# Seven block products over pairs of tiles in place of eight in two graph aggregations, and a first stage whose input comes in column layout

## The reference

```python
def _L1_gnn_ref(x, adj, W, b):
    agg = jnp.matmul(adj, x)
    out = jnp.matmul(agg, W.T) + b
    return jax.nn.relu(out)

def _L3_gnn_ref(x, adj, W, b):
    a = adj + jnp.eye(adj.shape[0], dtype=adj.dtype)
    d = jnp.sum(a, axis=1) ** (-0.5)
    a_norm = d[:, None] * a * d[None, :]
    support = a_norm @ x
    out = support @ W.T + b
    return jax.nn.relu(out)
...
x = _layernorm(x + _L1_gnn_ref(x, adj, L1_gnn_W, L1_gnn_b), axis=-1)
```

## Time and profile before

| | us |
|---|---|
| median of three runs | 2541.1 |
| lowest and highest | 2539.39, 2542.22 |
| the profiled execution, its own time | 2541.41 |
| its span, first to last instruction | 2539.6 |

### The profile page before, as it was taken

How to read it: one execution, slowest core, us unless ns; L and a number is a source line. 1 busy time by engine, 2 the same in 40 slices (tenths; PEclk the granted TensorE clock), 3 DMA queues, 4 the chain that set the end, 5 groups by cost and what they waited for, 6 DMA issues and landing times. The chain is left out here.

```text
span 2539.6 us, 67049 instructions
## 1 busy us (share of the span) xinstructions
PE 2424.1 (95%) x24988; PEld 1557.7 (61%) x24988; DVE 1545.9 (61%) x3013; ACT 1364.0 (54%) x2036; POOL 1148.7 (45%) x971
## 2 busy tenths in 40 slices
PE   7997999999999999999879997999999999979998
PEld 6885777777777777777634443774444555534443
DVE  4435998898888898888632222555555566633222
ACT  3335888888888888888623221324434444323222
POOL 0005888888888888888601232001111113310323
PEclk9998999999999999999989999999999999989999
DMA  3216999999999999999743654215666779733664
GB/s 130 65 62 129 183 195 185 188 193 181 190 193 178 187 193 184 191 188 185 123 137 118 213 199 158 100 37 138 175 183 181 203 207 233 178 128 101 211 213 140
DMA packets 783644, 417.41 MB, mean 164 GB/s; under 512 B 691296, under 2 KB 717664, under 8 KB 774496
## 3 DMA queue, kind: packets, MB, share of 16 engines
q1 hardware_dynamic: 783456, 414.62, 70.7%
HBM read 203.55 MB, written 40.84 MB: 96 GB/s over the span
## 5 line engine op out<-in xcount | busy, mean ns | idle before, releaser
L806 DVE CUSTOM_DVE_ANT_0 att_scores<-att_slots,att_adj 128x1024 f32<-128x1024 f32 x528 | 575.7, 1091 | 41.6 <-POOL att_part_low L627 14.5
L627 POOL TENSOR_TENSOR att_part_low<-att_scores,att_part_high 128x1024 f16<-128x1024 f32 x352 | 574.8, 1651 | 12.0 <-ACT att_part_high L790 1.1
L751 ACT ACTIVATE att_scores<-att_scores,att_nmax 128x1024 f32<-128x1024 f32 x528 | 552.4, 1047 | 28.2 <-DVE att_lifted L817 26.0
L672 PE MATMUL att_slots<-l_kk,att_q 128*128 128x512 f16 x2112 | 466.5, 356 | 15.5 <-DMA att_q<-q_rows 8.9
L1345 PE MATMUL a_ps<-l_y,a_adj 128*128 128x512 f16 x1936 | 421.2, 381 | 9.0 <-DVE a_adj L1359 4.7
L825 DVE TENSOR_TENSOR att_near_low<-att_ps_t,att_near_high 128x512 f16<-128x512 f32 x528 | 316.4, 599 | 37.6 <-ACT att_near_high L760 35.9
L760 ACT ACTIVATE att_near_high<-att_ps_t 128x512 f16<-128x512 f32 x528 | 258.2, 524 | 150.0 <-PE att_ps_t L682 137.3
L1345 PEld LDWEIGHTS a_ps<-l_y,a_adj 128*128 128x128 f16 x1936 | 190.0, 98 | 240.1 <-DVE a_adj L1359 5.2
L672 PEld LDWEIGHTS att_slots<-l_kk,att_q 128*128 128x128 f16 x2112 | 195.2, 98 | 173.4 <-DVE att_least L806 24.9
L1090 PE MATMUL edge_ps_o<-l_sup,edge_pt_high 128*128 128x512 f16 x968 | 287.9, 379 | 1.7 <-DMA edge_pt_low<-edge_part_low 1.7
L1330 ACT ACTIVATE a_adj<-l_adj 128x2816 f16<-128x2816 f32 x44 | 112.0, 2549 | 291.1 <-DMA l_adj<-in_adj_cols 271.1
(11 more groups left out here) (152 smaller groups left out, 3863.2 us busy)
## 6 DMA issues: line engine op xcount, KB each, us to landing
l_adj<-in_adj_cols SPq DMA_DIRECT2D x44, 1408.0 KB, 6.1
l_adj_tiles<-in_adj SPq DMA_DIRECT2D x22, 1354.0 KB, 6.1
att_adj<-in_adj SPq DMA_DIRECT2D x66, 384.0 KB, 4.2
p_x_in<-x SPq DMA_DIRECT2D x66, 256.0 KB, 2.6
att_q<-q_rows SPq DMA_DIRECT2D x44, 256.0 KB, 3.8
a_xres<-x SPq DMA_DIRECT2D x44, 256.0 KB, 2.8
p_x_in<-in_x SPq DMA_DIRECT2D x22, 256.0 KB, 2.7
q_rows<-l0w_q_halves SPq DMA_DIRECT2D x22, 256.0 KB, 2.1
```

Source lines behind the costliest of these rows:

```text
L627: nc.gpsimd.tensor_tensor(out=part[1][:, v, lo:lo + width], in0=sc[:, v, lo:lo + width], in1=part[0][:, v, lo:lo + width], op=ALU.subtract ...
L672: mm = nc.tensor.matmul(slots[:, slot, z:z + w], q[:, u, h % 2, a, h // 2, :], kk[:, h, lo + z:lo + z + w], start=a == 0, stop=a == 1)
L751: nc.scalar.activation(sc[:, v, lo:lo + width], sc[:, v, lo:lo + width], ACT.Exp, bias=nmax[:, v:v + 1], scale=-1.0).then_inc(exp_done, 1)
L806: nc.vector.tensor_tensor_reduce(out=sc[:, v, lo:lo + width], in0=slots[:, (NC * h + c) % 2, 0:width], in1=adj[:, u, lo:lo + width], scale ...
```

## The change

`aggregate` works on pairs of output tiles, m = 0 to 10. A pair's adjacency columns are a 2x2 grid by parity of the block and tile in the pair, y a 2x2 grid by parity of the tile and half of the columns. By Strassen's scheme seven products of block sums give the four quarters. ACT narrows both tiles of a pair into one of three buffers, DVE makes five sums of blocks (`combine`, each 11 blocks of 128, 1408 elements), PE runs seven products of 22 matmuls with 256 columns each, ACT copies four of the products from PSUM to SBUF, DVE puts the quarters together (`add`, eight additions of 256 columns), then come bias, residual and statistics of both tiles (`bias`). The second factor, seven combinations of quarters of y with high and low part, is made in p1 and p3: ACT evicts both tiles of a pair in float32 (`y32`), DVE makes the five sums, ACT and DVE write the high and low parts (`halves`). The loops of p1, p3, a1 and a3 are written out. In p0 the host gives x in column layout (`x_cols`): no transposes, ACT and DVE split it straight out of the loaded tile, and the second tile of x is loaded behind the key weights, ahead of the others.

```diff
+def each(eng, begin, end, step):
+    for t in range(begin, end):
+        step(t // 2, t % 2)
...
+                src = x_rows[bass.ds((2 * m + u), 1), :, :].rearrange("o p n -> (o p) n") if columns \
+                    else x_rows[bass.ds((2 * m + u) * P, P), :]
+                sp.dma_start(x_in[:, u, :], src).then_inc(x_loaded[u], 16)
...
             load(0, 0)
-            own.load(sp)
+            own.load(sp, slice(0, 2))
             load(0, 1)
+            own.load(sp, slice(2, None))
             late_w.load(sp)
...
+                if columns:
+                    return
...
+                        if combos is None:
+                            pe.wait_ge(out_low, nj * (2 * m + u - 2) + n + 1)
+                        else:
+                            pe.wait_ge(evicted, 2 * m + u - 1)
...
+            def halves(m, u):
+                t = 2 * m + u
+                act.wait_ge(made, t + 1)
+                if t > 1:
+                    act.wait_ge(out_low, 2 * m)
+                scale = V_S * XW if row_scale is None else row_scale[:, bass.ds(t, 1)]
+                slots = y32[:, 1::2, :] if u == 0 else y32[:, 0::2, :]
+                nc.scalar.activation(slots, ps_job[0][:, u, :].rearrange("p (c n) -> p c n", c=2), ACT.Copy,
+                                     scale=scale).then_inc(evicted, 1)
+                if u == 1:
+                    act.wait_ge(evicted, t + 1)
+                    nc.scalar.activation(combos[0][:, 5:7, m, :], y32[:, 1:3, :], ACT.Copy).then_inc(out_high, 1)
+                    act.wait_ge(y_summed, 3 * m + 3)
+                    nc.scalar.activation(combos[0][:, 0:5, m, :], sums[:, :, :], ACT.Copy).then_inc(out_high, 1)
...
+            def halves(m, u):
+                if u == 0:
+                    return
+                dve.wait_ge(evicted, 2 * m + 2)
+                if m > 0:
+                    dve.wait_ge(out_low, 2 * m)
+                nc.vector.tensor_tensor(out=sums[:, 0:2, :], in0=y32[:, 0:2, :], in1=y32[:, 2:4, :], op=ALU.add) \
+                    .then_inc(y_summed, 1)
+                nc.vector.tensor_tensor(out=sums[:, 2:4, :], in0=y32[:, 0:4:3, :], in1=y32[:, 1:3, :],
+                                        op=ALU.subtract).then_inc(y_summed, 1)
+                nc.vector.tensor_tensor(out=sums[:, 4, :], in0=y32[:, 1, :], in1=y32[:, 2, :], op=ALU.add) \
+                    .then_inc(y_summed, 1)
+                dve.wait_ge(out_high, 2 * m + 1)
+                nc.vector.tensor_tensor(out=combos[1][:, 5:7, m, :], in0=y32[:, 1:3, :], in1=combos[0][:, 5:7, m, :],
+                                        op=ALU.subtract).then_inc(out_low, 1)
+                dve.wait_ge(out_high, 2 * m + 2)
+                nc.vector.tensor_tensor(out=combos[1][:, 0:5, m, :], in0=sums[:, :, :], in1=combos[0][:, 0:5, m, :],
+                                        op=ALU.subtract).then_inc(out_low, 1)
...
-        a16 = s.sb("adj16", [P, 2, T, P], F16)
+        a16 = s.sb("adj16", [P, 3, 2, T, P], F16)
+        a_sum = s.sb("adj_sum", [P, 2, 5, T // 2, P], F16)
         xres = s.sb("xres", [P, 2, D])
-        act_in = s.sb("act_in", [P, D])
+        total, copied = s.sb("total", [P, 2, 2, D // 2]), s.sb("copied", [P, 2, 2, D // 2])
         norm = Norm(s)
-        ps = s.ps("ps", [P, 2, BANK])
+        ps = s.ps("ps", [P, 2, 4, 2, D // 2])
...
+            def load_adj(t):
+                if t > 1:
                     sp.wait_ge(narrowed, t - 1)
+                    sp.dma_start(a32[:, t % 2, :, :], columns_of(adj_cols, t)).then_inc(adj_loaded[t % 2], 16)
+            def load_x(t):
+                if t > 1:
                     sp.wait_ge(r_ready, t - 1)
+                sp.dma_start(xres[:, t % 2, :], x_rows[t * P:(t + 1) * P, :]).then_inc(xres_loaded[t % 2], 16)
+            load_adj(2)
+            load_adj(3)
+            load_x(0)
+            load_x(1)
+            for m in range(1, M):
+                if m < M - 1:
+                    load_adj(2 * m + 2)
+                    load_adj(2 * m + 3)
+                for u in range(2):
+                    load_x(2 * m + u)
+                    norm.store(sp, out_rows, m - 1, u)
+            norm.store(sp, out_rows, M - 1, 0)
+            norm.store(sp, out_rows, M - 1, 1)
...
+            def narrow(m):
+                for u in range(2):
+                    if m > 0:
+                        act.wait_ge(adj_loaded[u], 16 * m)
+                    if m > 2:
+                        act.wait_ge(summed, PRODUCTS * (m - 2))
+                    nc.scalar.activation(a16[:, m % 3, u, :, :], a32[:, u, :, :], ACT.Copy).then_inc(narrowed, 1)
+            for m in range(3):
+                narrow(m)
+            for m in range(M):
+                for n in range(2):
+                    act.wait_ge(summed, PRODUCTS * m + 2 + 4 * n)
+                    if m > 0:
+                        act.wait_ge(added, ADDS * m)
+                    nc.scalar.activation(copied[:, n, :, :], ps[:, m % 2, 2 * n, :, :], ACT.Copy) \
+                        .then_inc(copies, 1)
+                if m + 3 < M:
+                    narrow(m + 3)
...
+            for m in range(M):
+                pe.wait_ge(combined, 4 * (m + 1))
+                if m > 1:
+                    pe.wait_ge(added, ADDS * (m - 1))
+                s16, s2 = a16[:, m % 3, :, :, :], a_sum[:, m % 2, :, :, :]
+                a11, a22 = s16[:, 0, 0::2, :], s16[:, 1, 1::2, :]
+                factors = [(s2[:, 4, :, :], 4), (a22, 2), (s2[:, 0, :, :], 6), (s2[:, 2, :, :], 0),
+                           (a11, 3), (s2[:, 1, :, :], 5), (s2[:, 3, :, :], 1)]
+                for n, (a, c) in enumerate(factors):
+                    for k in range(M):
+                        for b in range(2):
+                            mm = nc.tensor.matmul(ps[:, m % 2, n // 2, n % 2, :], a[:, k, :], y[b][:, c, k, :],
+                                                  start=k == 0 and b == 0, stop=k == M - 1 and b == 1)
+                    mm.then_inc(summed, 1)
...
+            def combine(m):
+                s16, out = a16[:, m % 3, :, :, :], a_sum[:, m % 2, :, :, :]
+                dve.wait_ge(narrowed, 2 * m + 2)
+                if dcol is not None:
+                    for u in range(2):
+                        block_of = s16[:, u, 2 * m + u, :]
+                        nc.vector.tensor_tensor(out=block_of, in0=block_of, in1=ident[:, :], op=ALU.add) \
+                            .then_inc(diag_ready, 1)
+                    dve.wait_ge(diag_ready, 2 * m + 2)
+                if m > 1:
+                    dve.wait_ge(summed, PRODUCTS * (m - 1))
+                for u in range(2):
+                    op_of = nc.vector.tensor_tensor(out=out[:, u, :, :], in0=s16[:, u, 0::2, :],
+                                                    in1=s16[:, u, 1::2, :], op=ALU.add)
+                op_of.then_inc(combined, 1)
+                for n, (u, odd, v, odder, op) in enumerate(((0, 1, 1, 1, ALU.subtract), (1, 0, 0, 0, ALU.subtract),
+                                                            (0, 0, 1, 1, ALU.add))):
+                    nc.vector.tensor_tensor(out=out[:, 2 + n, :, :], in0=s16[:, u, odd::2, :],
+                                            in1=s16[:, v, odder::2, :], op=op).then_inc(combined, 1)
+            def add(m):
+                m5, m7, m6 = (ps[:, m % 2, n // 2, n % 2, :] for n in (2, 3, 6))
+                m1, m4, m3, m2 = (copied[:, n // 2, n % 2, :] for n in range(4))
+                c11, c12, c21, c22 = (total[:, n // 2, n % 2, :] for n in range(4))
+                if m > 0:
+                    dve.wait_ge(r_ready, 2 * m)
+                for n, (made, out, a, b, op, own) in enumerate((
+                        (2, c11, m1, m4, ALU.add, 0), (4, c11, c11, m5, ALU.subtract, 1), (4, c11, c11, m7, ALU.add, 2),
+                        (6, c12, m3, m5, ALU.add, 0), (6, c21, m2, m4, ALU.add, 0), (6, c22, m1, m2, ALU.subtract, 0),
+                        (6, c22, c22, m3, ALU.add, 6), (7, c22, c22, m6, ALU.add, 7))):
+                    dve.wait_ge(copies, 2 * m + (1 if made < 6 else 2))
+                    dve.wait_ge(summed, PRODUCTS * m + made)
+                    if own:
+                        dve.wait_ge(added, ADDS * m + own)
+                    nc.vector.tensor_tensor(out=out, in0=a, in1=b, op=op).then_inc(added, 1)
+            def bias(m, u):
+                t = 2 * m + u
+                scale = 1.0 / V_S if dcol is None else dcol[:, t:t + 1]
+                row = total[:, u, :, :].rearrange("p c n -> p (c n)")
+                dve.wait_ge(added, ADDS * m + (5 if u == 0 else ADDS))
+                nc.vector.scalar_tensor_tensor(out=row, in0=row, scalar=scale, in1=bias_row[:, :], op0=ALU.mult,
+                                               op1=ALU.add).then_inc(biased, 1)
                 dve.wait_ge(biased, t + 1)
                 dve.wait_ge(xres_loaded[u], 16 * m + 16)
                 norm.free(dve, m, u)
```

(21 more changed lines are left out.)

111 lines of the change are left out of this document (32 added, 79 removed).

## The result

The changed kernel takes 2800.9 us (median of four runs, 2795.86 to 2804.34), the kernel before in the same comparison 2541.3. The ratio is 1.102, with a 95% interval from 1.100 to 1.104: slower by 260 us. The profiled execution of it spans 2797.9 us, against 2539.6.

The account below looks back on a forecast made before the run. PE bound the kernel before; after, a serial ring of queues would pace the aggregations. From 2541.4 us, +179 for the aggregations with their ends, +56 for the projections and -14 for the first stage gave 2762, range 2720 to 2840.

Parts of the forecast that it names:

- PE gives back 24 us per aggregation: Aggregations: eleven pairs of 256-column matmuls take PE 185 us against 209, if nothing else sets the pace.
- The ring: Aggregations: store, next loads, narrowing, copies, adds, biases and block sums follow in series, 30.0 us per pair; PE needs 16.8.
- The last term, bias to store: Aggregation's ring: second tile's bias, statistics, POOL and the store's issue take 6.04 us, read from the earlier trace.
- A block sum of 0.89 us: Aggregations: a float16 DVE addition of 1408 elements, absent from the earlier trace, taken at 0.89 us.
- The rival that rested on the other rate: Aggregations: block sums at the float32 rate, 0.78 us more each, +78 us, 2840 us in all; chance 0.12.
- The end, +5.5 us: End of each aggregation: 11.3 us from the last matmul to POOL's last output, 5.8 before.
- The projections, +28 us each: Projections before the aggregations: PE's waits cost 24 us and a later end of the last pair 4, +56 in all.
- It waits 2.4 us, ten times: Each projection: PE waits for the input's low split, ready at 5.85 us but wanted at 3.47, 24 us in all.
- the second rival: Projections: the clock falls at each wait, 20 x 1.8 = 36 us more, 2798 us in all; chance 0.07.
- The first stage, -14 us: First stage: transposes gone, 9.2 us, and PE's first product 4.6 us earlier.
- The rivals of the other side: Aggregations and projections: reordered queues hide all, 2511 us, faster, decided at a ring of 16.8 us; chance 0.02.

Follow-up runs that it names:

- the split first: The changed kernel with ACT's and DVE's order altered in p1 and p3, the next tile's input split ahead of the combinations of y: 2717.0 us, ratio 1.068.
- the copies first: The changed kernel with ACT's copies of pair k+1 out of PSUM ahead of the narrowing of pair k+3 in both aggregations: 2692.0 us, ratio 1.058.
- both repairs: The changed kernel with adjacency loads one pair earlier and, in p1 and p3, the input's split ahead of y's combinations: 2507.8 us, ratio 0.985.

## Why the forecast was right, and where it was off

The forecast was 2762 us, with a range of 2720 to 2840. The measured 2800.9 lies in it, 39 above the sum: 32 of them arose in the two projections and 12 in a1, while attention and layer 2 were 5 shorter.

**PE gives back 24 us per aggregation: right,** and seen only where PE is the bound. The matmul of 256 columns runs every 0.109 us (16.81 us for 154), the value read off the line between 128 and 512 columns.

**The ring sets the pace: right, and shown.** Issuing the loads one pair earlier brought back 208 us; nothing else is altered by that edit. In a1 the ring was 31.2 us, forecast 30.0; in a3 30.4, forecast 30.65.

**The mis-sized terms of the ring.** From the store's issue to the second narrowing's start it was 11.6 us in the turn above, against 11.05. The last term, bias to store, was 7.0 us (1515.22 to 1522.23) against 6.04: DVE's 1.10 us and its 0.91 of waiting for POOL. The earlier trace rows was read where no block sum ran beside POOL, so it could not show this, and the forecast took it as it stood. The block sums offset part of it: 4.02 us instead of 4.45, since they too overlap their ends. The stage started 0.3 us earlier but pair 3 came at 68.4 us instead of 65.6. 2.8 at the start, and 7 turns of 1.2: 11 of the 12 us that a1 was over the forecast. In a3 pair 3 came at 67.7, as forecast (67.6), and the ring was 0.2 us shorter, so there the terms offset each other; which of them did was not looked into.

**A block sum of 0.89 us: right,** 0.884 to 0.888 in the rows above, against 1.67 by the float32 row. The rule cited in the forecast from the Trainium skill ("VectorE: DVE Perf Modes") gave an estimate of 0.88, and the trace agrees. (Scaled by length alone, the 1224 ns for 2048 elements would give 0.84; the 0.88 holds some start-up.) The rival that rested on the other rate is out: it would have shown some 8.4 us of sums per pair, where there are 4.

**The end, +5.5 us: right.** In a3 the last product ended at 2782.68 and POOL's last output at 2794.31, 11.6 us against the forecast's 11.3.

**The projections, +28 us each: wrong, +44.** The step that failed is the price of a pair, "It waits 2.4 us, ten times". The wait was right (2.32 us), the mechanism too, and where the clock stayed up the period was 8.55 us against 8.45 forecast. But the waits, all but one in each of p1 and p3, were followed by about 3.4 us at the 1.2 GHz level, 1.7 us more per pair. That was the second rival, priced at 1.8 us per wait and 2798 us in all; the measured 2801 is that rival's time. The price was not read well: the earlier trace rows give 1.4 us (5.16 less 3.8) for the slow start of a1, not 1.8, which is what the forecast took off the 210.78 us of a3. It had been given 0.07, for the reason that before shows the low clock only behind a wait of 4.26 us. With the terms of the forecast and this one, the sum is within 3 us of the measured time, though a part of that is luck: a1 was 12 us longer, attention and layer 2, which the change does not touch, together 5 shorter.

The Trainium skill ("TensorE: Matmul & The Clock Gate", "HAM oscillation — how this bites in real kernels") describes bursts of matmuls with waits of 3 to 5 us between them, each of which begins at the low clock. This trace shows the same, in most turns, with waits of 2.32 us and bursts of 7.9 us between them. The run with the split first shows what it is worth here.

**The first stage, -14 us: right,** -14.4 between the two traces, -16 and -20 in the two runs of it alone (ratios 0.993 and 0.992). The first product was to begin 4.6 us earlier; it began 3.8 earlier, at 11.55 against 15.38, because the second key weight came later than forecast:

```profile
10.18 1.22 DVE L127 SCALAR_TENSOR_TENSOR l0w_wk_low<-p_w_stage,l0w_wk_high 128x1024 f16<-128x1024 f32 x1 [1.61 <-ACT l0w_wk_high L122]
...
11.55 0.37 PE L94 MATMUL p_ps_job<-p_xt,l0w_wk_high 128*128 128x128 f16 x2 [11.55 <-DVE l0w_wk_low L127]
```

**The rivals of the other side** asked when the new order would hide everything: at a ring of less than 16.8 us. The runs show it from the other end. The ring never gets there by being shorter (23.7 us with the copies out of it); its loads have to be issued further ahead, behind the store of a pair earlier.

## What to carry to other kernels

When a change gives the bound engine less to do but writes new orders for the others, go round the queues once, from a load to the load that it releases, and add up the durations: a ring that is longer than the bound engine's work per turn is the new pace, whatever the busy shares say. The repair is rarely less work; it was the loads issued one pair earlier, and a split moved ahead of work that nobody waits for. A change in several parts should be run in parts as well: here one part was a gain of 16 to 20 us, and the others a loss of some 275 that became a gain of 17 to 28 once the queues were reordered.

Price each wait of TensorE inside a running stage with its clock too: here most waits of 2.3 us cost 4.0.

## What the runs showed of the hardware

**Two engines that slow each other.** While float16 sums of two SBUF operands ran on DVE, POOL's 128x512 operation took 3.57 us instead of 2.08, its one-column operations 0.70 and 1.09 instead of 0.19 and 0.56, and a DVE operation of two SBUF operands beside POOL 1.10 instead of 0.69 us. With the overlap removed all four went back. DVE's block sums kept their pace (2.49 us for three in both), so the slowing is uneven. With the copies first it fell the other way, after the first tile of a1: POOL's 128x512 operation kept its 2.08 us, and two DVE additions of 256 columns of two SBUF operands beside it took 0.92 us, in one turn 1.14, instead of 0.75. The Trainium skill ("GPSIMD Engine Reference", "Key points") says that GpSimd shares its SBUF interfaces with VectorE and contends with its instructions that have two SBUF inputs; the trace agrees, and the prices are those above.

**The clock.** In p1 and p3 of the changed kernel PE waited 20 times. Behind 18 of the waits, of 2.2 to 2.9 us, came some 3.4 us with a granted clock of 0.51; behind two, of 1.96 and 2.06 us, the clock stayed up. The length of a wait doesn't decide it alone. In p3 of the run with the loads a pair earlier the waits were as long, and five of nine turns ran at full clock, two of them behind a wait of 2.41 us. One of these two, and the turn after it, which lost its clock:

```profile
2294.28:2302.92 8.64, 6.23 (x33) 3.24 (x33) 5.01 (x7) 4.25 (x7) 0.00 (x0) 1.00 0.24 63
2302.92:2312.97 10.05, 7.91 (x33) 3.88 (x33) 5.01 (x7) 4.25 (x7) 0.00 (x0) 0.83 0.19 51
```

That stage took 113.5 us there instead of 120, in an execution that was 10 us under the run's median. What makes the difference between two such turns no run here shows; with these waits in it the time of a stage varies, and without them (both repairs) it doesn't lose its clock at all once it runs.

**Loads in pairs.** Adjacency loads issued some 0.5 us apart took 8.5 us to land (median of 18 in a1), single ones 6.0. Twice the data arrive in less than twice the time, but a ring that waits for both sees the longer one.
